# A Perceiver's second cross attention: where GpSimd's normaliser diagonals stand among the next batch's rows

## The chip, the cores and the metric

The program runs on one core of a Trainium2 chip, as one launch. The metric is the device time of an execution in microseconds; the shown figure is the median of three runs. A core has five engines that run their own instruction streams and meet only at semaphores: TensorE (PE in the profile, with its weight loads as PEld), VectorE (DVE), ScalarE (ACT), GpSimd (POOL) and SyncE (SP, which issues the DMAs here).

## The reference, cut to what matters

The model has two layers: cross attention, self attention and a mixture of experts; then a second cross attention, a decayed linear attention and a quantised feed-forward. The change lies in the second cross attention. For each of 16 batches it takes 1601 context rows and 64 latent rows of 128 numbers and does this:

```
xn     = layernorm(context) * ln1_w + ln1_b          # 1601 x 128
latn   = layernorm(latents) * ln2_w + ln2_b          # 64 x 128
k, v   = split(concat([xn, latn]) @ Wkv)             # 1665 keys, 16 heads of 64
weight = softmax((latn @ Wq) . k / 8)                # 64 queries x 1665 keys, per head
out    = (weight . v) @ Wo
```

## The kernel before, in words

**How the work is cut.** `cross_attention_1` (L2162) folds the key weights into the queries beforehand, so that the scores of a batch are queries times xn transposed, and the values are xn itself. A batch's 16 heads are worked as eight pairs of heads (128 query rows), one pair to a *slot*. A *body* `k` is two batches: `m=0` is batch 2k, `m=1` is batch 2k+1; 16 slots to a body, eight bodies. The 1665 keys are cut into four *chunks*: three of 512 (four tiles of 128 rows) and one of 129 (65 last context rows and the 64 latent rows).

**One slot on each engine** (`attend`, L117, each engine's own `body`). PE makes the scores of this slot's pair (L269, four chunks of three passes), then turns the probabilities of the pair before (L239, chunks 0 and 1), weighs values of a still earlier pair of slots (L2346 to L2348, 21 matmuls), and turns chunks 2 and 3. DVE takes the maxima of the scores (L373, L420) and the low halves of the turned probabilities (L382, L385); ACT takes the exponentials (L349) and the high halves (L331, L333).

**Jobs between.** `lay.jobs` (L2171, L2172) puts small jobs into set places of a slot, "b" inside the scores before their last chunk, "a" after the values and before the turns of chunks 2 and 3. All share one PSUM bank, `scratch`, one after another, and wait for `scratch_free`. In the second half of each batch they are, in this order: turn chunk 0 of the **next** batch's rows (`x_t` 0: slot 4 "a"), chunk 1 (slot 5 "b"), the normaliser of the **current** batch's first four pairs (`norm`: slot 5 "a"), chunk 2 (slot 6 "b"), chunk 3 (slot 7 "b"). A second `norm`, for the last four pairs, stands in slot 1 "a" of the following batch. In batches with `m=0` slot 3 "a" also holds `out`, the output projection of the body before (L2327, 32 matmuls).

**norm.** Every four slots DVE sums the denominators and inverts them (`denominators`, L389: `rden`, L396; this happens late in slot 4 and in slot 0 of the next batch). GpSimd splits `rden` into two halves and makes two 128x512 blocks of four diagonals each (`split_diag`, L2353: L2356, L2358, twice L2361). PE multiplies them by ones (`pe_norm`: L2366, L2367), ACT copies the result out (L314), and DVE uses it when it finishes the four pairs (L2458). PE's `norm` waits for `diag_done`.

**GpSimd's order.** GpSimd's stream is written out by hand in `attend`'s `body` (L201). For each batch it runs: `make_diag` of the batch before's second quad; `pool_prepare` (L2295); `make_diag` of the current batch's first quad; `pool_split` (L2304). `pool_prepare` splits the next batch's queries, makes the layer norm's factors when DVE has the statistics (slot 2), and calls `normed_rows` (L2251): 13 instructions that centre and scale the tiles (L2256), then for each of the four chunks a multiplication by the weight (L2263) and an addition of the bias (L2269), which gives `xn` and counts `xn_done`; for chunk 3 it also copies the latent rows (L2268). `pool_split` makes the high and low halves of the values (`split_rows`, L2271), which PE needs in slot 3 of the next batch.

**Who else waits for `xn_done`.** PE's `x_t` jobs, chunk by chunk; SyncE, which loads the context rows of the batch after the next when all four chunks are done (`sync_body`, L2226); and DVE's `means`. For batch 0 DVE calls `normed_rows` itself, before the first slot.

Of the kernel before, what the change touches and what calls it, by code (L numbers as in the profile page):

```python
# [37 lines left out]
CHUNKS = 4  # L38
# [1173 lines left out]
def wait_apart(engine, sem, count, waits):  # L1212


    engine.wait_ge(sem, count)
    engine.sem_inc(waits, 1)
# [945 lines left out]
def cross_attention_1(nc, g, dram):  # L2162
# [11 lines left out]
    with ExitStack() as ctx:  # L2174
        t = Named()
# [62 lines left out]
        def split_queries(pool, b, m):  # L2238
            wait_apart(pool, t.q_loaded, (b + 1) * 16, t.pool_waits)
            nc.gpsimd.tensor_copy(t.q_hi[m][:], t.q_raw[:]).then_inc(t.q_split, 1)  # L2240
            pool.wait_ge(t.q_split, 2 * b + 1)
            nc.gpsimd.tensor_tensor(t.q_lo[m][:], t.q_raw[:], t.q_hi[m][:].bitcast(F32), ALU.subtract).then_inc(t.q_split, 1)

        def factors(pool, b):

            pool.wait_ge(t.eps, 2 * (b + 1))
            nc.gpsimd.tensor_tensor(t.rstd[:], t.rstd[:], t.half[:], ALU.pow).then_inc(t.rstd_done, 1)
            pool.wait_ge(t.rstd_done, b + 1)
            nc.gpsimd.tensor_tensor(t.shift[:], t.shift[:], t.rstd[:], ALU.mult).then_inc(t.shift_done, 1)

        def normed_rows(eng, ops, b, m, first, waits):  # L2251

            wait_apart(eng, t.shift_done, b + 1, waits)
            for i in range(FULL + 1):
                rows = lay.tiles[i][0]
                ops.tensor_scalar(t.ctx[0:rows, i, :], t.ctx[0:rows, i, :], t.rstd[0:rows, i:i + 1], t.shift[0:rows, i:i + 1],  # L2256
                                  ALU.mult, ALU.add).then_inc(t.centred, 1)
            for c in range(CHUNKS):
                n = 4 if c < 3 else 1
                rows, tiles = (P if c < 3 else TAIL), slice(4 * c, 4 * c + n)  # L2260
                eng.wait_ge(t.centred, (FULL + 1) * b + 4 * c + n)
                w, bias = (v[0:rows].unsqueeze(1).broadcast_to([rows, n, D]) for v in (t.weight, t.bias))
                ops.tensor_tensor(t.ctx[0:rows, tiles, :], t.ctx[0:rows, tiles, :], w, ALU.mult).then_inc(t.weighted, 1)  # L2263
                eng.wait_ge(t.weighted, CHUNKS * b + c + 1)
                if c == 0 and not (isinstance(b, int) and b == 0):
                    eng.wait_ge(lay.own.half_taken, CHUNKS * b)
                if c == 3:
                    ops.tensor_copy(t.xn[0:SEQ, LAT, :], g.lat_rows[:, bass.ds(b, 1), :].rearrange("p o d -> p (o d)"))  # L2268
                ops.tensor_tensor(t.xn[0:rows, tiles, :], t.ctx[0:rows, tiles, :], bias, ALU.add).then_inc(t.xn_done, 1)  # L2269

        def split_rows(eng, ops, b, m, first, waits):  # L2271

            if not first:
                wait_apart(eng, lay.own.pv_done, CHUNKS * QUADS * (b - 1), waits)
            wait_apart(eng, t.xn_done, CHUNKS * (b + 1), waits)
            for c in range(CHUNKS):
                for rows, tiles in (((P, slice(4 * c, 4 * c + 4)),) if c < 3 else ((TAIL, slice(FULL, FULL + 1)), (SEQ, slice(LAT, LAT + 1)))):
                    last = ops.tensor_copy(t.v_hi[m][0:rows, tiles, :], t.xn[0:rows, tiles, :])
                last.then_inc(t.v_high, 1)
            for c in range(CHUNKS):  # L2280
                eng.wait_ge(t.v_high, CHUNKS * b + c + 1)
                for rows, tiles in (((P, slice(4 * c, 4 * c + 4)),) if c < 3 else ((TAIL, slice(FULL, FULL + 1)), (SEQ, slice(LAT, LAT + 1)))):
                    last = ops.tensor_tensor(t.v_lo[m][0:rows, tiles, :], t.xn[0:rows, tiles, :], t.v_hi[m][0:rows, tiles, :].bitcast(F32), ALU.subtract)
                last.then_inc(t.v_split, 1)
# [10 lines left out]
        def pool_prepare(pool, k, kind, m):  # L2295
            b = 2 * k + m + 1
            first = kind == "first" and m == 0
            if not first:
                pool.wait_ge(lay.own.scores_ready, (b - 1) * PAIRS * CHUNKS)
            split_queries(pool, b, (m + 1) % 2)  # L2300
            factors(pool, b)
            normed_rows(pool, nc.gpsimd, b, (m + 1) % 2, first, t.pool_waits)

        def pool_split(pool, k, kind, m):  # L2304
            split_rows(pool, nc.gpsimd, 2 * k + m + 1, (m + 1) % 2, kind == "first" and m == 0, t.pool_waits)

        lay.pool_start, lay.pool_prepare, lay.pool_split = pool_start, pool_prepare, pool_split

        def pe_start(pe):
# [76 lines left out]
        def x_low(dve, c, b, m):  # L2386
            cols = quad_chunk(c, KEYS)
            dve.wait_ge(lay.own.half_taken, CHUNKS * b + c + 1)
            nc.vector.tensor_tensor(t.x_lo[m][:, cols], lay.own.scratch[:, 0:cols.stop - cols.start], t.x_hi[m][:, cols].bitcast(F32),
                                    ALU.subtract).then_inc(lay.own.scratch_free, 1)  # L2390
# [13 lines left out]
        def statistics(dve, b, i):  # L2404

            if i == 0:
                dve.wait_ge(t.ctx_loaded, (b + 1) * 32)
            rows = lay.tiles[i][0]
            nc.vector.bn_stats(t.stats[0:rows, i, :], t.ctx[0:rows, i, :]).then_inc(t.stat, 1)

        def means(dve, b, tiles):

            wait_apart(dve, t.stat, (FULL + 1) * b + tiles[-1] + 1, t.waits)
            for i in tiles:
                rows = lay.tiles[i][0]
                nc.vector.bn_aggr(t.mean_var[0:rows, i, :], t.stats[0:rows, i, :]).then_inc(t.aggr, 1)
            if tiles[-1] == FULL:
                dve.wait_ge(t.aggr, (FULL + 1) * (b + 1))

                if not (isinstance(b, int) and b == 0):  # L2420
                    dve.wait_ge(t.xn_done, CHUNKS * b)
                nc.vector.tensor_scalar(t.rstd[:], t.mean_var[:, :, 1], LN_EPS, None, ALU.add).then_inc(t.eps, 1)
                nc.vector.tensor_scalar(t.shift[:], t.mean_var[:, :, 0], -1.0, None, ALU.mult).then_inc(t.eps, 1)

        def dve_start(dve):
            for v in t.x_hi + t.x_lo:
                nc.vector.memset(v[:, KEYS:KEYS + 1].bitcast(U32), 0).then_inc(t.pads_set, 1)
            nc.vector.memset(t.mean_var[:], 0.0).then_inc(t.pads_set, 1)
            dve.wait_ge(t.pads_set, 5)
            for i in range(FULL + 1):  # L2430
                statistics(dve, 0, i)
            means(dve, 0, list(range(FULL + 1)))
            dve.wait_ge(t.loaded, 32)
            normed_rows(dve, nc.vector, 0, 0, True, t.waits)
            for c in range(CHUNKS):
                x_low(dve, c, 0, 0)

# [23 lines left out]
        def dve_end(dve):  # L2461
# [3 lines left out]
            add_output(dve, BODIES - 1)  # L2465

        lay.dve_start, lay.dve_take, lay.dve_finish, lay.dve_extra, lay.dve_end = dve_start, dve_take, dve_finish, dve_extra, dve_end
        lay.dve_between = dve_between
        attend(nc, g, lay, ctx)
# [103 lines left out]
```

## Time and profile before

| | |
|---|---|
| median of three runs | 1780.35 us (1780.29, 1780.35, 1783.54) |
| the profiled execution | 1783.51 us, of which the profile's span is 1781.6 us |
| busy share of the span | PE 91%, PEld 77%, DVE 71%, ACT 54%, POOL 34% |
| the second cross attention | about 735 to 1697 us of the span |
| one batch of it | 58.4 us with `m=0`, 57.3 us with `m=1` |

Times in the rows are microseconds from the start of the span, or microseconds that something lasted. A row of the timeline has the start, the duration, the engine and line, and what was written and read; in brackets at its end stands how long the engine had been idle just before, and what ended that. Instructions that run on in a row on the same tile are merged ("x6"). Matmuls overlap, so the distance between two starts says more than a duration. Idle time that ended with "issue" is time for which the profile shows no releaser.

### The profile page before, as it was taken

The numbers are of one execution on the slowest core, as the hardware profiler recorded it, in microseconds if no ns is written. First come the engines' busy times: TensorE is split into PE (matmuls) and PEld (weight loads), VectorE is DVE, ScalarE is ACT, GpSimd is POOL, SyncE is SP. The second block draws the span as 40 slices with busy tenths as digits, with TensorE's granted clock in tenths as the row PEclk, the third lists the DMA queues.
The fourth block names the chain that finished last, engine by engine and source line by source line (L and its number), as shares of the span: only waits on it lengthen the run. The fifth ranks groups of instructions, "written<-read, shape, count | busy, mean of one in ns | idle before, by whom it ended". The sixth has DMA issues, their size and how long they took to land. (4 is left out here: it accounts for less than half of the span.)

```text
span 1781.6 us, 34512 instructions
## 1 busy us (share of the span) xinstructions
PE 1624.9 (91%) x13452; PEld 1375.8 (77%) x13452; DVE 1266.1 (71%) x2833; ACT 955.2 (54%) x1788; POOL 605.1 (34%) x855
## 2 busy tenths in 40 slices
PE   6999999999997998289999999999999999999964
PEld 4776767667676887178898998989989889899843
DVE  7677776766763776377777787777777777777587
ACT  3566665656552434156655566555655665556443
POOL 2000100101102231354457546554557446752110
PEclk8999999999998999699999999999999999999986
DMA  6534535344320011300000010010000000100000
GB/s 167 135 94 101 148 98 131 94 106 100 78 54 1 25 49 71 130 31 13 31 20 31 13 31 20 31 32 13 31 20 31 13 31 20 31 1 1 1 3 9
DMA packets 32689, 90.90 MB, mean 51 GB/s; under 512 B 8552, under 2 KB 17424, under 8 KB 32528
## 3 DMA queue, kind: packets, MB, share of 16 engines
q1 hardware_dynamic: 32528, 88.71, 18.7%
q8 instruction: 106, 1.74, 0.4%
q14 instruction: 55, 0.45, 0.1%
HBM read 40.43 MB, written 8.91 MB: 28 GB/s over the span
## 5 line engine op out<-in xcount | busy, mean ns | idle before, releaser
L382 DVE TENSOR_TENSOR c_p_lo<-c_turn_ps,c_p_hi 128x512 fp32r<-128x512 f32 x384 | 264.5, 689 | 187.6 <-ACT c_p_hi L331 187.5
L331 ACT ACTIVATE c_p_hi<-c_turn_ps 128x512 fp32r<-128x512 f32 x384 | 228.7, 596 | 248.2 <-PE c_turn_ps L239 246.0
L1020 DVE TENSOR_REDUCE a_chunk_max<-a_side_ps 128x1 f32<-128x512 f32 (+1 forms) x416 | 260.6, 665 | 96.3 <-PE a_side_ps L771 95.8
L2346 PE MATMUL c_pv_ps<-c_p_hi,c_v_lo 128*128 128x256 f32 (+2 forms) x896 | 267.6, 299 | 0.0
L349 ACT ACTIVATE c_prob<-c_score_ps,c_neg_max 128x1024 f32<-128x1024 f32 (+1 forms) x256 | 245.6, 959 | 36.2 <-DVE c_neg_max L420 36.2
L373 DVE TENSOR_REDUCE c_chunk_max<-c_score_ps 128x1 f32<-128x1024 f32 (+2 forms) x384 | 257.7, 725 | 9.2 <-PE c_score_ps L269 9.2
L239 PE MATMUL c_turn_ps<-consts,c_prob 128*128 128x128 f32 (+1 forms) x1792 | 246.0, 276 | 11.8 <-DVE c_p_lo L382 11.6
L2347 PE MATMUL c_pv_ps<-c_p_hi,c_v_hi 128*128 128x256 f32 (+2 forms) x896 | 249.9, 279 | 0.0
L2348 PE MATMUL c_pv_ps<-c_p_lo,c_v_hi 128*128 128x256 f32 (+2 forms) x896 | 249.3, 278 | 0.0
L931 ACT ACTIVATE a_prob<-a_st_ps 128x1024 f32<-128x1024 f32 (+1 forms) x224 | 214.1, 959 | 53.8 <-PE a_st_ps L755 53.1
L239 PEld LDWEIGHTS c_turn_ps<-consts,c_prob 128*128 128x128 f32 (+1 forms) x1792 | 194.9, 140 | 26.4 <-DVE c_p_lo L382 14.4
L269 PE MATMUL c_score_ps<-c_x_hi,c_q_hi 128*128 128x512 f32 (+1 forms) x512 | 195.6, 382 | 3.2 <-ACT c_prob L349 2.4
L269 PE MATMUL c_score_ps<-c_x_lo,c_q_hi 128*128 128x512 f32 (+1 forms) x512 | 187.6, 366 | 0.0
L269 PE MATMUL c_score_ps<-c_x_hi,c_q_lo 128*128 128x512 f32 (+1 forms) x512 | 187.5, 366 | 0.0
L2346 PEld LDWEIGHTS c_pv_ps<-c_p_hi,c_v_lo 128*128 128x128 f32 (+2 forms) x896 | 168.9, 189 | 8.9
L2347 PEld LDWEIGHTS c_pv_ps<-c_p_hi,c_v_hi 128*128 128x128 f32 (+2 forms) x896 | 170.1, 190 | 0.0
L755 PE MATMUL a_st_ps<-a_q_bd,a_stack 100*128 100x256 f32 (+1 forms) x832 | 168.5, 322 | 1.3 <-DVE a_q_bd L1030 1.2
L771 PE MATMUL a_side_ps<-a_stack,a_q_bd 96*128 96x512 f32 (+1 forms) x512 | 160.4, 390 | 9.3 <-DVE a_chunk_max L1020 3.6
L2348 PEld LDWEIGHTS c_pv_ps<-c_p_lo,c_v_hi 128*128 128x128 f32 (+2 forms) x896 | 168.6, 188 | 0.0
L755 PEld LDWEIGHTS a_st_ps<-a_q_bd,a_stack 100*128 100x128 f32 (+1 forms) x832 | 117.1, 188 | 29.7 <-issue 26.9
L804 PE MATMUL a_pv_ps<-a_prob,a_val 128*17 128x128 f32 (+1 forms) x3328 | 116.2, 274 | 0.7 <-ACT a_prob L931 0.6
L269 PEld LDWEIGHTS c_score_ps<-c_x_hi,c_q_hi 128*128 128x128 f32 x512 | 97.3, 190 | 19.8 <-ACT c_prob L349 2.5
(334 smaller groups left out, 2786.2 us busy)
## 6 DMA issues: line engine op xcount, KB each, us to landing
a_stack<-a_k_hi SPq DMA_DIRECT2D x128, 200.1 KB, 4.2
a_stack<-a_k_lo SPq DMA_DIRECT2D x64, 200.1 KB, 4.2
a_ctx<-in_ctx_dram SPq DMA_DIRECT2D x16, 768.0 KB
c_ctx<-in_ctx_dram SPq DMA_DIRECT2D x16, 768.0 KB
absorbed_queries<-b_q_out SPq DMA_DIRECT2D x16, 512.0 KB, 3.3
c_q_raw<-absorbed_queries SPq DMA_DIRECT2D x16, 512.0 KB, 3.3
w<-in_L_ffn_w_dram SPq DMA_DIRECT2D x2, 512.0 KB
fold_raw<-in_L_xattn_Wkv_dram SPq DMA_DIRECT2D x2, 512.0 KB
```

What stands on the lines that cost most here:

```text
L239: last = nc.tensor.transpose(turn_ps[c % 2][0:rows, P * i:P * i + P], prob[(s - 1) % 2][:, col:col + rows], ident)
L269: mm = nc.tensor.matmul(score_ps[:, cols], queries, keys_t[:, cols], start=(i == 0), stop=(i == len(passes) - 1))
L331: last = nc.scalar.activation(p_hi[u][:, 4 * c:4 * c + 4, P * j:P * j + P], turn_ps[c % 2][:].rearrange("p (t q) -> p t q", t=4), ACT.Copy)
L349: nc.scalar.activation(prob[s % 2][:, cols], score_ps[:, cols], ACT.Exp, bias=neg_max[:, s % 2:s % 2 + 1], accum_out=sums[:, (s // QUAD) % ...
L373: nc.vector.reduce_max(chunk_max[:, s % 2, c:c + 1], score_ps[:, maxima_of[c]], AX_X).then_inc(chunk_max_done, 1)
L382: last = nc.vector.tensor_tensor(p_lo[u][part], turn_ps[c % 2][:].rearrange("p (t q) -> p t q", t=4), p_hi[u][part].bitcast(F32), ALU.subt ...
L755: last = nc.tensor.matmul(st_ps[t % 2][0:rows, i, 256 * v:256 * v + 256], stack[:, m, 2 * u + v, col:col + rows], q_bd[m][:, 2 * u + v].re ...
L931: nc.scalar.activation(out, scores, ACT.Exp).then_inc(exp_done, 1)
L1020: nc.vector.reduce_max(out, rows, AX_X).then_inc(side_taken, 1)
L2346: nc.tensor.matmul(out, v_lo, lay.own.p_hi[u][0:rows, i, :], start=(i == 0), stop=False)
L2347: nc.tensor.matmul(out, v_hi, lay.own.p_hi[u][0:rows, i, :], start=False, stop=False)
L2348: last = nc.tensor.matmul(out, v_hi, lay.own.p_lo[u][0:rows, i, :], start=False, stop=(i == LAT))
```

## The change

`normed_rows` is cut in two: `centred_rows`, the wait and the 13 centring instructions, and `weighted_rows`, which does the weight and bias of the chunks that it is given. `pool_prepare` now ends with the weighted rows of chunks 0 and 1. Those of chunks 2 and 3 become the first thing in `pool_split`, behind the `make_diag` that stands between the two. No instruction is added or taken away, no wait is changed, and batch 0's rows on DVE keep their order.

```diff
-        def normed_rows(eng, ops, b, m, first, waits):
+        def centred_rows(eng, ops, b, waits):
             wait_apart(eng, t.shift_done, b + 1, waits)
             for i in range(FULL + 1):
                 ...
-            for c in range(CHUNKS):
+
+        def weighted_rows(eng, ops, b, chunks):
+            for c in chunks:
                 ...
             factors(pool, b)
-            normed_rows(pool, nc.gpsimd, b, (m + 1) % 2, first, t.pool_waits)
+            centred_rows(pool, nc.gpsimd, b, t.pool_waits)
+            weighted_rows(pool, nc.gpsimd, b, range(2))
         def pool_split(pool, k, kind, m):
+            weighted_rows(pool, nc.gpsimd, 2 * k + m + 1, range(2, CHUNKS))
             split_rows(pool, nc.gpsimd, 2 * k + m + 1, (m + 1) % 2, kind == "first" and m == 0, t.pool_waits)
-            normed_rows(dve, nc.vector, 0, 0, True, t.waits)
+            centred_rows(dve, nc.vector, 0, t.waits)
+            weighted_rows(dve, nc.vector, 0, range(CHUNKS))
```

## Rows read from the trace of the kernel before

**Rows 1.** Busy time by engine in one stretch; us, five engines, granted clock, DMA share, GB/s.
```profile
1000.00:1230.00 230.00, 226.26 (x1636) 206.16 (x1634) 172.59 (x407) 135.26 (x278) 127.83 (x176) 1.00 0.07 23
```
**Rows 2.** Waits from 735 to 1700; total us, times, longest us.
```profile
PEld c_scratch L2366 <- issue: 10.2, 8, 1.3
PE c_scratch L2366 <- POOL c_diag_lo L2361: 8.9, 8, 1.1
...
PE c_turn_ps L239 <- DVE c_p_lo L382: 11.6, 14, 1.3
```
**Rows 3.** Timeline of PE, slots 5 to 7 of a batch with m=1.
```profile
1199.91 0.28 PE L2348 MATMUL c_pv_ps<-c_p_lo,c_v_hi 128*128 128x256 f32 x1
1201.30 0.47 PE L2366 MATMUL c_scratch<-c_diag_hi,c_ones_r 128*128 128x512 f32 x1 [1.11 <-POOL c_diag_lo L2361]
...
1202.42 0.48 PE L269 MATMUL c_score_ps<-c_x_hi,c_q_hi 128*128 128x512 f32 x1
...
1204.59 0.60 PE L2321 MATMUL c_scratch<-consts,c_xn 128*128 128x128 f32 x4
...
1209.62 0.48 PE L269 MATMUL c_score_ps<-c_x_hi,c_q_hi 128*128 128x512 f32 x1
```
**Rows 4.** Timeline of PE, the same slots of a batch with m=0.
```profile
1144.13 0.28 PE L2348 MATMUL c_pv_ps<-c_p_lo,c_v_hi 128*128 128x256 f32 x1
1144.24 0.39 PE L2366 MATMUL c_scratch<-c_diag_hi,c_ones_r 128*128 128x512 f32 x1
...
1145.28 0.47 PE L269 MATMUL c_score_ps<-c_x_hi,c_q_hi 128*128 128x512 f32 x1
...
1147.44 0.60 PE L2321 MATMUL c_scratch<-consts,c_xn 128*128 128x128 f32 x4
...
1152.40 0.47 PE L269 MATMUL c_score_ps<-c_x_hi,c_q_hi 128*128 128x512 f32 x1
```
**Rows 5.** Timeline of POOL, the batch with m=1: chunks 1 and 2, diagonals.
```profile
1193.52 1.29 POOL L2269 TENSOR_TENSOR c_xn<-c_ctx,c_ln_b 128x512 f32<-128x512 f32 x1
1194.77 1.30 POOL L2263 TENSOR_TENSOR c_ctx<-c_ctx,c_ln_w 128x512 f32<-128x512 f32 x1
...
1198.57 0.18 POOL L2356 CAST c_rden_hi<-c_rden 128x4 fp32r<-128x4 f32 x1
...
1200.11 1.04 POOL L2361 TENSOR_TENSOR c_diag_lo<-consts,c_rden_lo 128x512 fp32r<-128x512 f32 x1
1201.10 2.21 POOL L2278 CAST c_v_hi<-c_xn 128x512 fp32r<-128x512 f32 x5
```
**Rows 6.** Timeline of DVE, the batch with m=1, and slot 0 after it.
```profile
1193.23 0.18 DVE L396 RECIPROCAL c_rden<-c_den 128x4 f32<-128x4 f32 x1
...
1198.69 0.68 DVE L2389 TENSOR_TENSOR c_x_lo<-c_scratch,c_x_hi 128x512 fp32r<-128x512 f32 x1
1199.67 0.69 DVE L382 TENSOR_TENSOR c_p_lo<-c_turn_ps,c_p_hi 128x512 fp32r<-128x512 f32 x1 [0.30 <-ACT c_p_hi L331]
...
1220.81 0.67 DVE L2409 BATCH_NORM_STATS2 c_stats<-c_ctx 128x6 f32<-128x128 f32 x3
```
**Rows 7.** Timeline of DVE, the batch with m=0.
```profile
1137.45 0.18 DVE L396 RECIPROCAL c_rden<-c_den 128x4 f32<-128x4 f32 x1
...
1142.89 0.68 DVE L2389 TENSOR_TENSOR c_x_lo<-c_scratch,c_x_hi 128x512 fp32r<-128x512 f32 x1
1143.87 0.69 DVE L382 TENSOR_TENSOR c_p_lo<-c_turn_ps,c_p_hi 128x512 fp32r<-128x512 f32 x1 [0.30 <-ACT c_p_hi L331]
```
**Rows 8.** Timeline of POOL, the batch with m=0: chunk 1 done.
```profile
1135.10 1.29 POOL L2269 TENSOR_TENSOR c_xn<-c_ctx,c_ln_b 128x512 f32<-128x512 f32 x1
```
**Rows 9.** Busy time in two microseconds with the load of context rows; columns as above.
```profile
1200.00:1202.00 2.00, 0.89 (x6) 0.59 (x5) 0.36 (x1) 0.41 (x2) 2.00 (x4) 1.00 0.86 332
```
**Rows 10.** Timeline of PEld, norm's first weight load, with m=0 and m=1.
```profile
1144.13 0.19 PEld L2366 LDWEIGHTS c_scratch<-c_diag_hi,c_ones_r 128*128 128x128 f32 x1
...
1201.27 0.19 PEld L2366 LDWEIGHTS c_scratch<-c_diag_hi,c_ones_r 128*128 128x128 f32 x1 [1.28 <-issue]
```

## The prediction, made before the changed kernel was run

> **What bounds the kernel now.** I read the busy time by stretch first. In the middle of the second cross attention PE is busy 226.26 of 230 us at a granted clock of 1.00, DVE 172.59 and POOL 127.83 [rows 1]: PE sets the end, and only what PE waits for can be won. So I read PE's waits next. Past the stage's start two releasers leave PE idle again and again: the low halves of the probabilities (11.6 us in 14 waits) and the diagonals: the first matmul of the normaliser waited eight times for GpSimd's second diagonal block, 8.9 us, 1.1 us each [rows 2]. Then I read the timeline of one of these waits and of a batch that has none. With m=1, PE's last value matmul starts at 1199.91, the normaliser at 1201.30 and the next scores at 1202.42 [rows 3]; with m=0 the same three are at 1144.13, 1144.24 and 1145.28 [rows 4]. The batch with m=0 has the output projection in slot 3, so its PE comes later, and GpSimd is ready in time. The eight are therefore the batches with m=1 that prepare another batch, seven, and batch 0, whose body has no output projection yet.
>
> GpSimd's timeline shows why it is late: it goes from chunk 1 (done when chunk 2 starts, 1194.77) through chunks 2 and 3 and takes up the diagonals at 1198.57; they are done when the next work starts, at 1201.10 [rows 5]. But `rden` was there at 1193.23 + 0.18 = 1193.41 [rows 6]. The diagonals wait behind rows that PE takes only at 1204.59 [rows 3].
>
> **The change, part by part.** *The diagonals move ahead of chunks 2 and 3.* They take 1201.10 - 1198.57 = 2.53 us [rows 5]. With m=1 GpSimd reaches them at 1194.77, 1.36 us after `rden` came [rows 5, 6], so it doesn't wait, and they are done at 1197.30. PE wants them when its last value matmul is out, at about 1199.91 + 0.11 = 1200.02 (the 0.11 is that of m=0) [rows 3, 4]. They are 2.7 us early, and the wait goes whole.
>
> *What one wait is worth.* From the last value matmul to the next scores: 2.51 us with the wait [rows 3], 1.15 us without [rows 4]; the difference is 1.36 us. That is more than the idle 1.11 us, because behind a wait the first matmuls stand further apart. Eight times: 10.9 us. The lower bound is the idle time alone, 8.9 us [rows 2]. The upper one adds what slot 6 takes longer with m=1 than with m=0: 1209.62 - 1202.42 = 7.20 against 1152.40 - 1145.28 = 7.12 [rows 3, 4], 0.08 us, which may be an echo of the wait: 8 x 1.44 = 11.5 us. I take 10.9, since the batch with m=0 is the same sequence without the wait.
>
> The extra 0.25 us lies partly in the weight load: with m=0 it starts 0.11 us ahead of its matmul, with m=1 only 0.03 us ahead, after 1.28 us idle [rows 3, 4, 10]. The Trainium skill ("TensorE: Matmul & The Clock Gate", section "Architectural detail: the array is 16× 32×32, not 1× 128×128") says that PE can pull weight loads ahead of matmuls in flight. By that rule the constant ones would have been loaded during the wait, only the idle 1.11 us would come back, and the sum would be 8.9 us; this trace shows the load held behind the wait with its matmul.
>
> *What is late next.* At that point PE also needs the shared PSUM bank, free when DVE has chunk 1's low half: 1198.69 + 0.68 = 1199.37 against 1200.02 [rows 3, 6]. With m=0 the same margin is 1144.24 - (1142.89 + 0.68) = 0.67 us and nothing waits [rows 4, 7]. The turns of chunks 2 and 3 that follow need DVE's low halves; the last starts at 1199.67, 0.35 us ahead of PE's coming to the normaliser, and with m=0 at 1143.87, 0.37 us ahead [rows 3, 4, 6, 7]. So the freed batch falls onto a pattern that runs without a wait today.
>
> *Chunks 2 and 3 move behind the diagonals.* Chunk 2 takes what it takes now: weight and bias start 1.37 us apart and last 1.29 us, about 2.66 us (the second row of chunk 1's kind ends 1.29 us after its start) [rows 5]. With m=1 it is done at 1197.30 + 2.66 = 1199.96; PE turns it at 1204.59 - 1.36 = 1203.23 [rows 3]: 3.3 us to spare. With m=0 GpSimd is free at 1135.10 + 1.29 = 1136.39 and now waits for `rden` until 1137.45 + 0.18 = 1137.63 [rows 7, 8]: a new idle time of 1.2 us. Diagonals at 1140.2, chunk 2 at 1142.8, wanted at 1147.44 [rows 4]: 4.6 us to spare. Chunk 3 is wanted a slot later still. Cost: nothing, as long as these covers hold.
>
> *What is queued behind.* Behind the diagonals on GpSimd now stand chunks 2 and 3 and then the value halves, as before; those end where they ended with m=1 and 1.2 us later with m=0, and PE needs them only three slots into the next batch. SyncE's load of the batch after the next waits for chunk 3, so it starts 2.5 us later. Its burst is now at 1200 to 1202 (0.86 of the DMA engines, 332 GB/s) [rows 9], and DVE first reads these rows at 1220.81 [rows 6]: some 14 us remain. Cost: nothing. The burst now falls beside running matmuls, as it does with m=0 already.
>
> **The sum.** The profiled execution took 1783.51 us (span 1781.6 and 1.9 around it); less 10.9 that is 1772.6. The median of the runs shown is 3.2 us below that execution, at 1780.35; I take the difference from the median: **1769.5 us**, 0.6% less. By the bounds, 1768.8 to 1771.5.
>
> **The rivals.**
> *Half comes back as another wait.* PE gains 1.36 us on DVE and ACT in slot 5, and the margins there are 0.35 to 0.65 us. If the turns or the shared bank held PE for half of what it gains, 5.4 us are left: 1774.9. For it: low halves are PE's other wait, 11.6 us in 14 [rows 2]. Against it: none of the seven later batches with m=0, with equal margins, waits there [rows 4, 7].
> *Nothing moves.* GpSimd was only the last of two releasers, or `rden` comes so late that the diagonals are done no earlier: 1780.35. The first needs a second releaser after 1201.15, and the bank is free at 1199.37; the second is refuted by 1193.41 [rows 6].
> *Slower: chunk 2 becomes late.* Between `rden` and PE's turn of chunk 2 lie 9.8 us in both kinds of batch, into which GpSimd must now fit 2.53 + 2.66 = 5.2 us. If it ran half as fast beside a busy DVE, the 5.2 extra would exceed the spare 3.3 (seven batches with m=1) by 1.9 and the spare 4.6 (eight with m=0) by 0.6: 13.3 + 4.8 = 18.1 us of new waits in slot 6, less the 10.9 won: 1787.6. It decides from about 4.5 us of extra time on; below that the change still wins. For it: GpSimd and DVE both work through the stretch. Against it: the weight and bias instructions last 1.29 and 1.30 us where DVE is at work and where it isn't [rows 5].
> The Trainium skill ("SBUF — State Buffer", section "Who interferes with whom") lets a DVE instruction block GpSimd if it reads two inputs from SBUF or runs in a two-port mode. The DVE instructions beside the moved work read at least one input from PSUM, so by that rule too this rival is unlikely; the equal durations agree.
>
> **How the numbers follow.** Forecast 0.82; half comes back 0.07; nothing moves 0.06; slower 0.05. A difference below 0.2% (3.6 us) can't be told from no change here. The first two cases are faster by more: 0.89; the third is the same: 0.06; the fourth slower: 0.05. The range starts at 1767.5, the 1768.8 of the upper bound less what two executions of a kernel differ anyway (the runs shown lie 3.3 us apart), and ends at 1775.0, which takes in the lower bound, a median that falls at the profiled execution's height (1772.6), and the half case.
>
> **What would show it.** Right: after the change the normaliser's first matmul follows the last value matmul by 0.11 us with m=1 too, PE's wait for the diagonals is gone from the list, and the batches with m=1 last some 55.9 us and not 57.3. On GpSimd the diagonals stand between two pairs of weight and bias rows; with m=0 about 1.2 us of idle time for `rden` stands ahead of them. Wrong: a wait of PE's turns for low halves in slot 5, or of the turn of chunk 2 for GpSimd in slot 6, or a DVE that waits for its context rows in slot 0.

## The result, and the profile after

The changed kernel took 1772.28 us, the kernel before 1782.33 us (medians of 20 runs each). The ratio is 0.9949, with a 95% interval of 0.9937 to 0.9962: by it the changed kernel is 9.1 us faster, between 6.8 and 11.2 (the two medians lie 10.1 us apart). Forecast were 10.9 us less and a time of 1769.5 us. The saving that was forecast lies inside the interval; the time is 2.8 us off, of which 2.0 come from the kernel before, which took 1782.33 us in these runs and not 1780.35.

Busy time in the same stretch as [rows 1], in the same columns: PE is busy 2.2 us more of the 230 (two of the old waits of 1.11 us lay in such a stretch), and the clock is the same.
```profile
1000.00:1230.00 230.00, 228.50 (x1647) 208.26 (x1646) 174.71 (x419) 136.50 (x282) 128.15 (x177) 1.00 0.08 25
```
PE's waits, the list of [rows 2]: the two rows of the diagonals are gone, and the one of the low halves is nearly as it was.
```profile
PE c_turn_ps L239 <- DVE c_p_lo L382: 11.4, 13, 1.3
```
PE's timeline in a batch with m=1, which answers to [rows 3]. The normaliser is now at L2371; it follows the last value matmul after 0.12 us, and the next scores come 1.15 us after that matmul, where they came after 2.51.
```profile
1192.73 0.28 PE L2353 MATMUL c_pv_ps<-c_p_lo,c_v_hi 128*128 128x256 f32 x1
1192.85 0.39 PE L2371 MATMUL c_scratch<-c_diag_hi,c_ones_r 128*128 128x512 f32 x1
...
1193.88 0.48 PE L269 MATMUL c_score_ps<-c_x_hi,c_q_hi 128*128 128x512 f32 x1
...
1196.06 0.60 PE L2326 MATMUL c_scratch<-consts,c_xn 128*128 128x128 f32 x4
...
1201.08 0.48 PE L269 MATMUL c_score_ps<-c_x_hi,c_q_hi 128*128 128x512 f32 x1
```
GpSimd in the same batch ([rows 5]): chunk 1, the diagonals, chunk 2, chunk 3. The diagonals are done at 1190.08, when the next work starts, 2.77 us before PE takes them at 1192.85; chunk 2 is done at 1191.44 + 1.30 = 1192.74, 3.3 us before its turn at 1196.06.
```profile
1186.30 1.29 POOL L2272 TENSOR_TENSOR c_xn<-c_ctx,c_ln_b 128x512 f32<-128x512 f32 x1
1187.53 0.19 POOL L2361 CAST c_rden_hi<-c_rden 128x4 fp32r<-128x4 f32 x1
...
1189.08 1.04 POOL L2366 TENSOR_TENSOR c_diag_lo<-consts,c_rden_lo 128x512 fp32r<-128x512 f32 x1
1190.08 1.29 POOL L2266 TENSOR_TENSOR c_ctx<-c_ctx,c_ln_w 128x512 f32<-128x512 f32 x1
1191.44 1.30 POOL L2272 TENSOR_TENSOR c_xn<-c_ctx,c_ln_b 128x512 f32<-128x512 f32 x1
```
GpSimd in the batch with m=0 that comes before it ([rows 8]): the new idle time ahead of the diagonals, 1.57 us.
```profile
1127.85 1.29 POOL L2272 TENSOR_TENSOR c_xn<-c_ctx,c_ln_b 128x512 f32<-128x512 f32 x1
1130.71 0.19 POOL L2361 CAST c_rden_hi<-c_rden 128x4 fp32r<-128x4 f32 x1 [1.57 <-DVE c_rden L396]
```
DVE in the batch with m=1 ([rows 6]), and the first read of the next context rows. The last low half starts 0.36 us ahead of the normaliser, and PE does not wait for it; the rows are read at 1212.28.
```profile
1191.51 0.68 DVE L2394 TENSOR_TENSOR c_x_lo<-c_scratch,c_x_hi 128x512 fp32r<-128x512 f32 x1
1192.49 0.69 DVE L382 TENSOR_TENSOR c_p_lo<-c_turn_ps,c_p_hi 128x512 fp32r<-128x512 f32 x1 [0.30 <-ACT c_p_hi L331]
...
1212.28 0.67 DVE L2414 BATCH_NORM_STATS2 c_stats<-c_ctx 128x6 f32<-128x128 f32 x3
```
The load of those rows ([rows 9]) now runs beside busy matmuls (PE is the second figure), 14 us ahead of that read.
```profile
1196.00:1198.00 2.00, 2.00 (x19) 1.94 (x18) 1.74 (x4) 1.16 (x3) 2.00 (x4) 1.00 0.77 315
```

Counted from the first scores of slot 2 to those of the next batch's slot 2, each of the seven batches with m=1 lasts 55.9 us, where it lasted 57.2 to 57.3; one with m=0 still lasts 58.4. The durations of batches below are counted in the same way.

### The profile page after: what moved, and what is told of

The parts are those of the page before. It is cut to its first block and busy times, and to the rows that moved or that the text cites. A ratio compares the mean times of both kernels' runs of the same rounds, so it can differ in the third digit from the quotient of the medians.

```text
span 1768.8 us, 34512 instructions
## 1 busy us (share of the span) xinstructions
PE 1619.7 (92%) x13452; PEld 1372.4 (78%) x13452; DVE 1267.2 (72%) x2833; ACT 955.1 (54%) x1788; POOL 605.2 (34%) x855
## 5 line engine op out<-in xcount | busy, mean ns | idle before, releaser
L373 DVE TENSOR_REDUCE c_chunk_max<-c_score_ps 128x1 f32<-128x1024 f32 (+2 forms) x384 | 257.8, 725 | 10.1 <-PE c_score_ps L269 10.1
L239 PE MATMUL c_turn_ps<-consts,c_prob 128*128 128x128 f32 (+1 forms) x1792 | 246.5, 277 | 11.7 <-DVE c_p_lo L382 11.4
```

What stands on the lines that cost most here:

```text
L239: last = nc.tensor.transpose(turn_ps[c % 2][0:rows, P * i:P * i + P], prob[(s - 1) % 2][:, col:col + rows], ident)
L373: nc.vector.reduce_max(chunk_max[:, s % 2, c:c + 1], score_ps[:, maxima_of[c]], AX_X).then_inc(chunk_max_done, 1)
```

## The experiments

Two theories stood against each other. *The theory:* eight waits of PE for the diagonals go, each worth 1.36 us, and nothing else matters, as long as each chunk is ready when PE turns it. *The rival:* the order of the rows or the later load of the context rows gives the gain, or part of it comes back. In the cuts of the edits `...` marks lines left out; each edit is made to the changed kernel.

**e1: the new order in half of the batches.**
```diff
-            weighted_rows(pool, nc.gpsimd, b, range(2))
+            weighted_rows(pool, nc.gpsimd, b, range(2 if first or m == 1 else CHUNKS))
 ...
-            weighted_rows(pool, nc.gpsimd, 2 * k + m + 1, range(2, CHUNKS))
+            if m == 1 or kind == "first":
+                weighted_rows(pool, nc.gpsimd, 2 * k + m + 1, range(2, CHUNKS))
```


> The new order only where a batch with m=1 is worked on, and in batch 0; the seven other batches with m=0 keep the old order. Theory (the gain is eight waits of PE for the diagonals, 1.36 us each, all of them in these batches): the whole gain stays, 9 to 11 us below the kernel before; PE waits nowhere for the diagonals, and GpSimd's idle time ahead of the diagonals with m=0 (1.6 us) is gone without any effect on the time. Rival (the order helps in all fifteen batches, for instance by a later load of the context rows): about half of the gain, 5 us.


Measured: 1772.49 us beside 1781.41 for the kernel before, ratio 0.9951 (0.9934 to 0.9968): 8.7 us less, the whole gain. PE has no wait for the diagonals. In the batches with m=0 GpSimd takes up the diagonals without a pause again, and a batch lasts 58.44 us as before. So the new order in the seven batches with m=0 gives nothing, and GpSimd's new idle time there costs nothing.

**e2: the diagonals one chunk later.**
```diff
-            weighted_rows(pool, nc.gpsimd, b, range(2))
+            weighted_rows(pool, nc.gpsimd, b, range(3))
 ...
-            weighted_rows(pool, nc.gpsimd, 2 * k + m + 1, range(2, CHUNKS))
+            weighted_rows(pool, nc.gpsimd, 2 * k + m + 1, range(3, CHUNKS))
```


> The diagonals stand behind chunk 2 instead of behind chunk 1, so only chunk 3 is moved behind them. Theory: they are done 1.2 us earlier than in the kernel before (at 1199.95 on its clock, PE wants them at 1200.02), which is just enough: 9.5 to 11 us below the kernel before, with a wait of at most 0.1 us per batch left. Rival (the diagonals must come as early as can be): 2 to 6 us below.


Measured: 1771.32 us beside 1781.41, ratio 0.9943 (0.9923 to 0.9962): 10.2 us less. The timeline of PE shows how close it is: the normaliser starts 0.14 us after the last value matmul and its first matmul lasts 0.47 us, as it does behind a wait, but no idle time is left.
```profile
1192.27 0.28 PE L2353 MATMUL c_pv_ps<-c_p_lo,c_v_hi 128*128 128x256 f32 x1
1192.41 0.47 PE L2371 MATMUL c_scratch<-c_diag_hi,c_ones_r 128*128 128x512 f32 x1
```
Moving one small chunk, 1.2 us of GpSimd's work, was enough. A batch with m=1 lasts 55.98 us here and 55.94 in the changed kernel, so coming earlier still is worth 0.04 us a batch.

**e3: the diagonals one chunk earlier.**
```diff
-            weighted_rows(pool, nc.gpsimd, b, range(2))
+            weighted_rows(pool, nc.gpsimd, b, range(1))
 ...
-            weighted_rows(pool, nc.gpsimd, 2 * k + m + 1, range(2, CHUNKS))
+            weighted_rows(pool, nc.gpsimd, 2 * k + m + 1, range(1, CHUNKS))
```


> The diagonals stand behind chunk 0, ahead of chunks 1, 2 and 3. Theory (GpSimd's order must follow the order in which PE takes things): with either kind of batch GpSimd then waits for the inverted denominators until 0.65 us after PE begins to turn chunk 0, makes the diagonals (2.53 us) and chunk 1 (2.66 us), which is done 5.85 us after that begin; PE wants to turn chunk 1 at 3.25 us after it. So chunk 1 comes 2.6 us late in fifteen batches: with 0.25 us for the start after a wait 43 us of new waits, less the 10.9 won: some 30 us above the kernel before, no wait for the diagonals. Rival (earlier is better, or PE's slot absorbs the wait): 5 to 11 us below.


Measured: 1829.84 us beside 1782.22, ratio 1.0268 (1.0245 to 1.0291): 48 us more, where some 30 were expected. The waits are the ones forecast, 2.7 to 2.8 us in each of fifteen batches:
```profile
PE c_scratch L2326 <- POOL c_xn L2272: 41.7, 15, 2.8
```
From scores to scores slot 5 lasts some 10.21 us in nine batches, 2.98 more than without a wait, and 15 x 2.98 = 45 us. In the six others it lasts 11.7 to 13.1, together 12 us more. What sets these six apart is the granted clock: over ten microseconds around the wait it averages 0.71 to 0.83 there and 1.00 in the nine, because it fell to 0.50 (1.2 of 2.4 GHz) towards the end of the wait or just behind it. Busy time by two microseconds, columns as in [rows 1], around the wait that ends at 917.74:
```profile
914.00:916.00 2.00, 0.93 (x5) 0.41 (x3) 2.00 (x4) 0.00 (x0) 2.00 (x3) 1.00 0.00 0
916.00:918.00 2.00, 0.26 (x2) 0.29 (x3) 0.20 (x1) 0.00 (x0) 1.92 (x3) 0.72 0.00 0
918.00:920.00 2.00, 2.00 (x11) 2.00 (x10) 0.45 (x2) 0.60 (x1) 1.92 (x2) 0.50 0.00 0
...
922.00:924.00 2.00, 2.00 (x12) 2.00 (x12) 0.94 (x2) 1.29 (x4) 2.00 (x6) 0.58 0.71 215
```
and around an equal wait in the next batch, which ends at 979.34 and where the clock stayed:
```profile
978.00:980.00 2.00, 0.66 (x7) 0.69 (x7) 0.00 (x0) 0.00 (x0) 2.00 (x2) 1.00 0.00 0
980.00:982.00 2.00, 2.00 (x20) 2.00 (x19) 1.01 (x3) 1.79 (x3) 1.92 (x3) 1.00 0.05 12
```
So waits and clock give 45 + 12 = 57 us, less the 10.9 won: 46, against 48 measured. The expectation had the waits right and left out the clock.

**e4: the new order, with the diagonals as late as before.** `fill` makes multiplications of constants into a tile that nothing reads, each behind the one before (its own lines are left out here).
```diff
             weighted_rows(pool, nc.gpsimd, b, range(2))
+            fill(pool, (4, 4, 4, 2))
```


> The new order, with four extra multiplications on GpSimd (3.95 us, into a tile that nothing reads) ahead of the diagonals, so that with m=1 they are done when they were done in the kernel before, and chunks 2 and 3 stay behind them. Theory (only the time at which the diagonals are done counts): the gain is gone, -1 to +2 us against the kernel before, with eight waits of about 1.2 us for the diagonals and no wait for chunk 2 (0.8 us to spare). Rival (the gain is from the order of the rows or the later load): 9 to 11 us below stay.


Measured: 1783.65 us beside 1781.41, ratio 1.0009 (0.9993 to 1.0024): the gain is gone. The wait is back, for the diagonals alone:
```profile
PE c_scratch L2384 <- POOL c_diag_lo L2379: 8.3, 7, 1.2
```
In PE's timeline such a wait shows 1.19 us of idle time, and the slot lasts 8.66 us and not 7.22: 1.44 us, again 0.25 more than the idle time. (In batch 0, the eighth, the slot is only 0.2 us longer, with no idle time shown: its slot 3 lasted 7.92 us and not 6.81, at a granted clock of 0.57 from 774 to 778, so PE came 1.1 us later to diagonals that were 1.2 us late.)
```profile
1199.15 0.28 PE L2366 MATMUL c_pv_ps<-c_p_lo,c_v_hi 128*128 128x256 f32 x1
1200.61 0.47 PE L2384 MATMUL c_scratch<-c_diag_hi,c_ones_r 128*128 128x512 f32 x1 [1.19 <-POOL c_diag_lo L2379]
```
Chunks 2 and 3 still stand behind the diagonals, and the load of the context rows is at least as late as in the changed kernel; neither gives anything.

**e5: the new order, with chunks 2 and 3 later.**
```diff
+            fill(pool, (4, 4, 4, 4, 2))
             weighted_rows(pool, nc.gpsimd, 2 * k + m + 1, range(2, CHUNKS))
```


> The new order, with five extra multiplications on GpSimd (5.05 us, into a tile that nothing reads) behind the diagonals, ahead of chunk 2. Theory (PE turns chunk 2 in slot 6; 3.3 us are to spare in the eight batches of m=1's kind and 4.6 us in the seven others): chunk 2 comes 1.8 us and 0.4 us late, with 0.25 us for the start after a wait 8 x 2.05 + 7 x 0.65 = 21 us of new waits, less the 10.9 won: 8 to 12 us above the kernel before. Rival (chunk 2 has slack enough or PE makes the wait good elsewhere): 5 to 11 us below.


Measured: 1792.42 us beside 1781.41, ratio 1.0063 (1.004 to 1.0086): 11.2 us more. PE now waits in all fifteen batches, in slot 6, for chunk 2:
```profile
PE c_scratch L2339 <- POOL c_xn L2274: 16.9, 15, 1.7
```
With m=1 slot 6 lasts 9.00 to 9.06 us and not 7.20, with m=0 8.05 and not 7.12: 1.8 and 0.9 us each. Batch 0 was expected to wait like those with m=1 and waits like those with m=0, 0.58 us: its slot 3 lasted 7.85 us and not 6.81, at a granted clock that fell there too, so PE came 1.0 us later. The cover that the prediction named is real. PE's waits are 1.67 us with m=1 and 0.67 with m=0, near the 5.05 us of the delay less the cover in the changed kernel, 3.32 us with m=1 and 4.35 with m=0 (chunk 2 is done at 1135.91 there and turned at 1140.26); 3.3 and 4.6 were forecast.

**after_again and e6: what is left.** The remaining wait of PE comes from DVE in slot 2, which has five of the 13 tiles' statistics and makes what GpSimd's factors need.
```diff
-                statistics(dve, 2 * k + m + 1, 4 * n + c)
+                statistics(dve, 2 * k + m + 1, 5 * n + c)
 ...
-                for i in range(4 * n + 3, 4 * n + 4 + n // 2):
+                end = min(5 * n + 5, FULL + 1)
+                for i in range(5 * n + 3, end):
                     statistics(dve, b, i)
-                means(dve, b, list(range(4 * n, 4 * n + 4 + n // 2)))
+                means(dve, b, list(range(5 * n, end)))
```


> The changed kernel, and DVE makes the statistics of the next batch's 13 tiles in portions of 5, 5 and 3 over slots 0 to 2 instead of 4, 4 and 5, to take away what is left of PE's waits: 0.75 us in slot 3 of the seven batches with m=1, for low halves that DVE makes late after slot 2. DVE's slot 2 gets 0.6 us shorter. Theory: most of the wait goes, and the time falls 3 to 6 us below the changed kernel, 13 to 16 us below the kernel before. Rival (slots 0 and 1 of DVE become late instead): the same as the changed kernel or up to 5 us above it.


Measured: 1766.81 us beside 1782.22 for the kernel before, ratio 0.9913 (0.9895 to 0.993), and beside 1770.87 for the changed kernel on the same chip: 4.1 us below it (six runs from 1765.97 to 1768.97 beside seven from 1768.94 to 1779.77). In the list of [rows 2] PE keeps six of the thirteen waits of this kind, four at the stage's start and two at its end.
```profile
PE c_turn_ps L239 <- DVE c_p_lo L382: 6.1, 6, 1.3
```
Slot 3 with m=1 lasts 6.64 us and not 7.29; seven times that is 4.6 us.

> The changed kernel once more, for its time beside the other two on the same chip: 9 to 11 us below the kernel before; and, if batch 0 was short of its gain in the first profile because the granted clock fell there before the diagonals were due, a batch 0 that has the 1.36 us too wherever the clock does not fall.


Measured: 1770.87 us beside 1782.22, ratio 0.994 (0.9919 to 0.9961): 10.7 us less. Batch 0 gained next to nothing in this profile too (56.40 us after 56.54); its slot 2 lasts 7.85 us here, at a granted clock of 0.52 from 771.8 to 775.0, and 6.65 in the kernel before. In e1, which treats batch 0 in the same way, that slot lasts 6.64 and the batch 55.20, so there the gain of 1.34 us is whole.

## Why the prediction was right

*The removed wait.* Right: e4 makes the diagonals late again and brings the old time back, with no other new wait of PE, and e1 puts the whole gain in the batches that were named.

*Its size, 1.36 us and not the idle 1.11.* Right: 57.30 - 55.94 = 1.36 us for a batch, and e4's waits show the same extra of 0.25. Where the extra lies, the prediction had only in part. With the wait the normaliser starts 1.39 us after the start of the last value matmul [rows 3], without it 0.11 [rows 4]: 1.28 of the 1.36 us. The idle time counts only 1.11 of these, because it starts at the end of that matmul, 0.28 us after its start, where a normaliser that need not wait starts while that matmul still runs. So 0.17 us of the extra is lost overlap. The other 0.08 lies behind the normaliser's start: 1.12 us to the scores [rows 3] and 1.04 [rows 4], with a first matmul of 0.47 us and not 0.39. The held weight load would explain these 0.08 us: in e2, where no idle time is left, the load starts 0.03 us ahead of its matmul as behind the wait, and the matmul lasts 0.47 us too. In the changed kernel the load starts 0.11 us ahead:
```profile
1192.74 0.19 PEld L2371 LDWEIGHTS c_scratch<-c_diag_hi,c_ones_r 128*128 128x128 f32 x1
```
The Trainium skill ("TensorE: Matmul & The Clock Gate", section "Architectural detail: the array is 16× 32×32, not 1× 128×128") says that PE can pull weight loads ahead of matmuls in flight; this row, where the last value matmul is still running, agrees. The 8.9 us that the prediction put beside that rule were too low an estimate: by the reading above, a load made during the wait would have spared about 0.08 us of each, and 8 x 1.28 = 10.2 us would still come back. The interval of the total takes in 8.9, 10.2 and 10.9 alike; the single batches, with 1.36 us each, decide.

*Eight times.* Seven times in this profile. Batch 0 lasted 56.45 us, where it lasted 56.54: its slot 5 won 1.34 us, and slot 3, before any diagonal was due, lost 1.11. The granted clock says why. The first row is of the changed kernel at that place, the second of e1:
```profile
772.00:775.40 3.40, 3.06 (x9) 2.48 (x10) 2.29 (x12) 1.21 (x4) 1.77 (x1) 0.51 0.00 0
```
```profile
773.00:776.40 3.40, 3.01 (x18) 2.62 (x19) 3.22 (x13) 1.24 (x4) 1.72 (x1) 1.00 0.00 0
```
The clock fell there in some executions and not in others, after waits that the change doesn't touch. In six of the nine traces here (both of the changed kernel, e2 to e5) slot 2 or 3 of batch 0 lasts 7.8 to 7.9 us with a lower clock in it; in the kernel before, e1 and e6 neither does. Why in which, no run settles, and with one trace of the kernel before it isn't shown how often it falls there. From the start of slot 2 of batch 0 to that of slot 7 of batch 15 the kernel before took 900.32 us, the changed one 890.76 and e1 889.51: 9.6 and 10.8 us less. The profiled execution's own time fell by 12.8 us (1783.51 to 1770.75); 3.1 of that came before the stage's first matmul (744.34 and 741.28), where nothing was changed.

*What is late next.* Nothing, as forecast: margins and durations after are those of the batch with m=0 before, so none of the gain came back in slot 5. The 0.08 us of slot 6, the upper bound's addition, stayed (1201.08 - 1193.88 = 7.20), so it was no echo of the wait.

*The moved chunks.* 3.3 us to spare were forecast and measured with m=1; e5 used them up, and e3 shows the price one place further. GpSimd's new idle time with m=0 was put at 1.2 us and is 1.57, mainly since GpSimd starts 0.26 us after DVE's last instruction for it ends; it costs nothing (e1). The rival of a slower GpSimd did not come: chunk 2's weight and bias last 1.29 and 1.30 us in their new place. Two details of that rival were wrong and changed nothing. One DVE instruction beside the moved work, the reduction of the maxima (L420, 0.16 us), reads SBUF alone, if with one input only. And by the rival's own counts, seven batches less 3.3 us and eight less 4.6, it decides from 4.7 us of extra time on, not from 4.5. The range's lower end, 1767.5, is 1.3 us below 1768.8 and not the 3.3 us named beside it.

## What to carry to other kernels

Where the bounding engine waits for a helper engine, read the helper's order against the order in which its results are taken, and move the late result ahead only past work that is needed later: here one chunk (1.2 us) was enough, and one place too far made the kernel 48 us slower than before. The same sequence without the wait, elsewhere in the same trace, prices the wait better than its idle time, which leaves out the overlap that the wait destroys. When the wait is gone, read the list of waits again: the next one gave 4 us for the same kind of edit.

## What was not expected of the hardware

In six of fifteen waits of PE of 2.7 to 2.8 us the granted clock fell to 0.50, the lower of the two levels, for some microseconds, and the wait cost 4.4 to 5.8 us instead of 3.0 (e3); in the nine others the clock stayed at 1.00. What parts the six from the nine, no run shows. Behind the waits of 1.1 to 1.2 us (the kernel before, e4) and 1.7 us (e5) in the steady part, from 780 to 1650, it stayed at 1.00 too; in batch 0 it fell in six of the nine traces, behind waits of 0.9 to 1.3 us. The 20 runs of the changed kernel spread from 1769.0 to 1784.4 us, and the spread goes with the clock: the run of 1784.43 had a mean granted clock of 0.953, the three shortest 0.964 to 0.969.
